# Narrow projection columns carried through V, and token records by one-hot products, in an attention and expert-routing kernel

## The reference, cut to what matters

```python
# x: (4, 256, 32, 32) -> four images of 1024 tokens, 256 channels
q, k, v = Wq x + bq, Wk x + bk, Wv x + bv            # 32, 32 and 256 rows
x = alpha * v @ softmax(q.T @ k).T + x               # per image
t = tokens(x)                                        # (4, 1024, 256)
n = layernorm(t)
prods = n @ proxy.T                                  # 16 proxies
y = cumsum(prods[..., None] * n[..., None, :], axis=tokens)
t = t + sum_p softmax(prods / 4)[p] * y[p]
n = layernorm(t)
logits = n @ gate_w.T                                # 8 experts, the best 2 of each token
top_w = softmax(top2(logits))
t = t + sum_e combine[e] * (gelu(n @ w1[e] + b1[e]) @ w2[e] + b2[e])
```

## Time and profile before

| | us |
|---|---|
| median of three runs (lowest, highest) | 883.59 (874.88, 887.9) |
| the profiled execution | 888.49 |
| its span, first to last instruction | 886.7 |
| stage A ends, stage B begins | about 219.7 |
| stage B's last residual addition (L822) begins | 386.0 |
| stage C's first layer-1 matmul | 437.95 |

### The profile page before, as it was taken

The page is one execution under the profiler, slowest core; times in us unless marked ns, Lnnn a source line. Parts: engine busy times, 40 slices in busy tenths (PEclk is TensorE's granted clock), DMA queues, the critical chain, the costliest instruction groups (busy, mean ns, idle before and its releaser), DMA issues.

```text
span 886.7 us, 18873 instructions
## 1 busy us (share of the span) xinstructions
PE 791.0 (89%) x5745; PEld 720.2 (81%) x5746; DVE 468.3 (53%) x982; ACT 324.8 (37%) x588; POOL 420.8 (47%) x405
## 2 busy tenths in 40 slices
PE   4998989897899999961299999999999999999993
PEld 3887978787567666631299999999999999999993
DVE  3777878877335365643045454454545444454541
ACT  2764747375233334220132333323233332223330
POOL 2474745456112366447324555445555544555332
PEclk9999999999655597865599999999999999999998
DMA  8576594856311111220117565265755626555222
GB/s 292 181 291 285 180 418 159 331 213 225 135 48 48 48 48 48 72 65 8 54 32 238 144 190 180 43 228 142 234 144 182 184 42 231 142 142 142 25 25 27
DMA packets 47724, 130.03 MB, mean 147 GB/s; under 512 B 7104, under 2 KB 37184, under 8 KB 43072
## 3 DMA queue, kind: packets, MB, share of 16 engines
q1 hardware_dynamic: 30288, 104.74, 31.7%
q0 software_dynamic: 16032, 19.49, 12.8%
q10 hardware_dynamic: 1360, 5.24, 1.6%
HBM read 186.52 MB, written 47.79 MB: 264 GB/s over the span
## 4 chain that ended last, share of the span: by engine, by line
PE 48%; DMA 1%; issue 1%; POOL 1%; DVE 0%; POOLq 0%; ACT 0%; DVEq 0%
PE ps_h L68 8%; PE ps_h L69 8%; PE ps_h L70 8%; PE ps_y L70 8%; PE ps_y L69 8%; PE ps_y L68 8%; PE ps_x L1331 2%; DMA out_tok<-y,to_row 0%; POOL out_tok L1218 0%; DMA records<-places 0%; DMA x_rows<-normed,from_row 0%; POOLq L1139 0%; DVE yb L1292 0%; DVE xtl L1278 0%; ACT xth L1244 0%
## 5 line engine op out<-in xcount | busy, mean ns | idle before, releaser
L1253 ACT ACTIVATE g<-ps_h,bias 128x256 f32<-128x256 f32 x288 | 120.7, 471 | 282.6 <-PE ps_h L70 282.6
L1218 POOL DMA_INDIRECT out_tok<-y,to_row x72 | 124.5, 1730 | 155.7 <-DVE y L1299 134.3
L68 PE MATMUL ps_h<-xth,wbuf 128*128 128x256 f32 x576 | 164.7, 286 | 3.3 <-issue 1.8
L68 PE MATMUL ps_y<-wbuf,gl 128*128 x576 | 165.6, 288 | 0.0
L69 PE MATMUL ps_h<-xtl,wbuf 128*128 128x256 f32 x576 | 164.4, 285 | 0.0
L70 PE MATMUL ps_h<-xth,wbuf 128*128 128x256 f32 x576 | 164.3, 285 | 0.0
L70 PE MATMUL ps_y<-wbuf,gh 128*128 x576 | 163.2, 283 | 0.0
L69 PE MATMUL ps_y<-wbuf,gh 128*128 x576 | 163.0, 283 | 0.0
L68 PEld LDWEIGHTS ps_h<-xth,wbuf 128*128 128x128 f32 x576 | 112.0, 195 | 3.9 <-issue 2.1
L69 PEld LDWEIGHTS ps_h<-xtl,wbuf 128*128 128x128 f32 x576 | 112.1, 195 | 0.0
L70 PEld LDWEIGHTS ps_h<-xth,wbuf 128*128 128x128 f32 x576 | 112.0, 194 | 0.0
(11 more groups left out here) (189 smaller groups left out, 1403.3 us busy)
## 6 DMA issues: line engine op xcount, KB each, us to landing
wbuf<-wsplit SPq DMA_DIRECT2D x71, 2048.0 KB, 8.8
wsplit<-wbuf SPq DMA_DIRECT2D x14, 2048.0 KB, 12.0
wraw<-in_w SPq DMA_DIRECT2D x16, 1024.0 KB, 7.5
xraw<-in_x_ch ACTq DMA_DIRECT2D x5, 1024.0 KB, 11.0
tok<-in_x_tok SPq DMA_DIRECT2D x1, 4096.0 KB, 17.0
out_tok<-tok SPq DMA_DIRECT2D x8, 512.0 KB
normed<-x SPq DMA_DIRECT2D x8, 512.0 KB, 2.9
x_rows<-normed,from_row POOLq DMA_INDIRECT x72, 3.2
```

The lines of the kernel that those rows point to most:

```text
L68: eng.matmul(out, ll, rh, start=first, stop=False)
L1218: pool.indirect_dma_start(out=out, out_offset=bass.IndirectOffsetOnAxis(ap=to_row[:, par, s:s + 1], axis=0), in_=y[:, par, s, :], in_offse ...
L1253: last = act.activation(g[:, f, :], ps_h[:, q, f % 2, :], ACT.Gelu_apprx_tanh, bias=bias1[:, bass.ds(e, 1), f:f + 1].rearrange("p a f -> p ...
```

## The change

**In stage A** the proxies and gates are put behind V's weights. A new `extend` multiplies Wv by the 24 proxy and gate columns, so V's projection has 304 columns: 256 of V, 24 of V times proxy and gate, and 24 of x times proxy and gate. `weigh` now has 280 columns, and `tok` 280 per tile, so that the residual addition leaves the unnormed products of each token with proxies and gates beside the token. The statistics of the first norm are taken tile by tile in stage A (`statistics(g)`, `mean_var`); since the norm is a scale and a shift of a token, the normed products are a scale of the raw ones plus a shift times column sums (`Tokens.products`, on GpSimd, in three batches of 24, 4 and 4 tiles, the third in stage B), and their softmax follows (`softmax_in`, `exponential`, `softmax_out`). Four small transfers are put ahead of the others on SyncE's queue. V's projection alternates between two PSUM regions in another order. GpSimd gets a copy per part of V.

**In stage B** the transposes of normed tokens and both projections are gone. The four images' products are turned together by two transposes (`turn`), the matrices come from one matmul of 512 columns (`attend`), and the state and output have 264 columns: the 8 gate products ride along, and the logits are those less a mean times the gates' sums (`logits`). Operands that had 16 rows or columns are padded to 128. The indirect record transfers are gone: VectorE makes one-hot tiles in bf16, 8 of 256 columns (`cell`) and 16 of 128 (`lane_tile`, `lane_part`), and TensorE adds up 16 products of them per chunk in PSUM (`record`), from which `decode` makes `records` in SBUF at the end. The shares go into `normed` as 8 more columns (GpSimd's `combine`). The counts move from VectorE to GpSimd. The chunk loop has one more round at the end.

**In stage C** the load of `places` is gone, gathered rows have 264 elements, and VectorE copies each unit's share out of them (`keep_share`).

```diff
+EXT = NP + E
+CW = C + EXT
+VW = CW + EXT
+XW = C + E
+REST = IT // 2
...
+    def products(self, pool, fixed, lo, hi, n):
...
+        pool.wait_ge(self.mv_d, n + 1)
+        pool.tensor_tensor(shift, self.mv[:, lo:hi, 0], fixed.minus_one[:, :].to_broadcast([P, m]), ALU.mult)
+        pool.tensor_tensor(inv, self.mv[:, lo:hi, 1], fixed.eps[:, :].to_broadcast([P, m]), ALU.add).then_inc(self.inv_step, 1)
+        pool.wait_ge(self.inv_step, n * 6 + 1)
+        pool.tensor_tensor(inv, inv, fixed.minus_half[:, :].to_broadcast([P, m]), ALU.pow).then_inc(self.inv_step, 1)
+        pool.wait_ge(self.inv_step, n * 6 + 2)
+        pool.tensor_tensor(shift, shift, inv, ALU.mult).then_inc(self.inv_step, 1)
+        pool.tensor_tensor(prods, prods, wide(inv, NP), ALU.mult)
+        pool.wait_ge(self.inv_step, n * 6 + 3)
+        pool.tensor_tensor(spare, each(self.sums[:, 0:NP], NP), wide(shift, NP), ALU.mult).then_inc(self.inv_step, 1)
+        pool.tensor_tensor(gated, each(self.sums[:, NP:EXT], E), wide(shift, E), ALU.mult)
+        pool.wait_ge(self.inv_step, n * 6 + 4)
+        pool.tensor_tensor(prods, prods, spare, ALU.add).then_inc(self.prods_d, 1)
+        pool.wait_ge(self.prods_d, n + 1)
+        pool.tensor_tensor(spare[:, :, 0:E], gates, wide(inv, E), ALU.mult).then_inc(self.inv_step, 1)
+        pool.wait_ge(self.inv_step, n * 6 + 5)
+        pool.tensor_tensor(gated, gated, spare[:, :, 0:E], ALU.add).then_inc(self.inv_step, 1)
+
...
+BATCHES = ((0, NT - IT), (NT - IT, NT - REST), (NT - REST, NT))
...
+            sp.dma_start(wv_nat, wv.rearrange("(k p) m -> p k m", p=P)).then_inc(ext_in, 16)
+            sp.dma_start(wv_raw[:, :, CW:CW + NP], proxy_t.rearrange("(k p) n -> p k n", p=P)).then_inc(ext_in, 16)
+            sp.dma_start(wv_raw[:, :, CW + NP:VW], gate_t.rearrange("(k p) n -> p k n", p=P)).then_inc(ext_in, 16)
+            sp.dma_start(bv_col, bv_t).then_inc(ext_in, 16)
...
                 for ch in range(4):
+                    js = slice(2 * ch, 2 * ch + 2)
                     pool.wait_ge(v_hi, done(b * 4 + ch))
-                    pool.tensor_tensor(vl[:, 2 * ch:2 * ch + 2, :], vf[:, ch % 2].rearrange("p (j c) -> p j c", j=2),
-                                       vh[:, 2 * ch:2 * ch + 2, :].bitcast(F32), ALU.subtract).then_inc(v_ok, 1)
+                    pool.tensor_copy(mine[:, js, :], vf[:, ch % 2, :, CW:VW])
+                    pool.tensor_tensor(vl[:, js, :], vf[:, ch % 2, :, 0:CW], vh[:, js, :].bitcast(F32),
...
-                        if not more and (par, part) == (1, 0):
-                            pool.wait_ge(norm_set, 3)
-                            norm1.scale_and_shift(pool, 0)
+                        if not more and par == 0:
+                            tok.products(pool, fixed, *BATCHES[part], part)
...
+                def statistics(g):
+                    wait_apart(dve, added, done(g))
+                    dve.bn_stats(tok.stat[:, bass.ds(g, 1), :].rearrange("p a c -> p (a c)"),
+                                 tok.t[:, bass.ds(g, 1), 0:C].rearrange("p a c -> p (a c)")).then_inc(tok.stat_d, 1)
...
+                def routing_weights(it):
+
+                    if it < B - 1:
+                        tok.mean_var(dve, it * IT, (it + 1) * IT, 0, it == B - 2)
+                    if it == REST:
+                        tok.mean_var(dve, *BATCHES[1], 1)
+                        tok.softmax_in(dve, *BATCHES[0], 0)
+                    if it == IT - 2:
+                        tok.softmax_out(dve, *BATCHES[0], 0)
+                        tok.softmax_in(dve, *BATCHES[1], 1)
+                    if it == IT - 1:
+                        tok.softmax_out(dve, *BATCHES[1], 1)
 
...
                 def project_v(ch):
-                    if ch == 2:
+                    if ch == 1:
                         pe.wait_ge(added, done(b * IT - 1))
-                    dst = ps_pt[1][:, ch * HALF:(ch + 1) * HALF] if ch < 2 else ps_o[ch - 2][:, :]
+                    if ch >= 2:
+                        pe.wait_ge(v_full, done(b * 4 + ch - 2))
                     for j in range(2):
+                        dst = ps_pt[1][:, j * HALF:j * HALF + VW] if ch % 2 == 0 else ps_o[:, j, 0:VW]
                         rows = slice((2 * ch + j) * P, (2 * ch + j + 1) * P)
                         for k in range(KT):
-                            last = mm3(pe, dst[:, j * C:(j + 1) * C], (xh[:, k, rows], xl[:, k, rows]),
+                            last = mm3(pe, dst, (xh[:, k, rows], xl[:, k, rows]),
                                        (wvh[:, k], wvl[:, k]), k == 0, k == KT - 1)
...
+            def prepare(c, par):
+
+                pool.wait_ge(turn_mm, done(c - 1))
+                pool.wait_ge(state_mm, done(c - 2))
+                pool.wait_ge(out_mm, done(c - 2))
+                pool.wait_ge(x1_d, done(c - 2))
+                if isinstance(c, int):
+                    pool.wait_ge(tok.weights_d, 2 if c < REST else 3)
+                else:
+                    pool.wait_ge(tok.weights_d, 3)
+                prods = chunk_of(tok.t[:, :, :], c)[:, :, C:C + NP]
+                pool.tensor_copy(prod_in[:, :, 0:NP], prods)
+                pool.tensor_copy(weight_in[:, :, 0:NP], chunk_of(tok.weights[:, :, :], c))
+                pool.tensor_copy(prod[:, par].rearrange("p (b n) -> p b n", b=B)[:, :, 0:NP], prods)
+                pool.tensor_copy(xn[:, par, :, C:XW], chunk_of(tok.gated[:, :, :], c))
+                pool.tensor_copy(inv_shift[:, par], tok.inv_shift[:, :, :].rearrange("p s (b c) -> p s b c", b=B)[
+                    :, :, :, bass.ds(c, 1)].rearrange("p s b a -> p s (b a)")).then_inc(prep_d, 1)
...
+            def mark_cells(c, par):
+
+                dve.wait_ge(spot_d, done(c))
+                dve.wait_ge(rec_mm, done(c - 2))
+                for kb in range(KB):
+                    last = dve.tensor_scalar(cell[:, par, kb, :], column_id[:, :], spot[:, 1, kb:kb + 1], None, ALU.is_equal)
+                last.then_inc(cell_d, 1)
+                wait_apart(dve, tile_d, done(c - 1))
+                for k in range(2):
+                    for b in range(B):
+                        mine = spot[:, 0, k * B + b:k * B + b + 1]
+                        dve.tensor_scalar(lane_tile[:, par, k * B + b, :], lane_id[:, :], mine, tile_no[:, b:b + 1],
+                                          ALU.is_equal, ALU.mult)
+                        last = dve.tensor_scalar(lane_part[:, par, k * B + b, :], lane_id[:, :], mine, part_id[:, 0:1],
+                                                 ALU.is_equal, ALU.mult)
...
-            def scatter(c, par):
-
-                wait_apart(pool, record_d, done(c))
-                for k, b in [(k, b) for k in range(2) for b in range(B)]:
-                    pool.indirect_dma_start(
-                        out=places, out_offset=bass.IndirectOffsetOnAxis(ap=place[:, par, k, b:b + 1], axis=0),
-                        in_=record[:, par, k, b, :], in_offset=None).then_inc(record_out[par], 16)
...
+                then(dve.tensor_copy(number[:, :], ps_rec[:, CELLS:2 * CELLS]), 1)
+                dve.scalar_tensor_tensor(out=empty[:, :], in0=ps_rec[:, 0:CELLS], scalar=0.0, in1=padding_id[:, :],
+                                         op0=ALU.is_equal, op1=ALU.mult)
+                then(dve.scalar_tensor_tensor(out=number[:, :], in0=ps_rec[:, 0:CELLS], scalar=float(P), in1=number[:, :],
+                                              op0=ALU.mult, op1=ALU.add), 2)
+                then(dve.scalar_tensor_tensor(out=records[:, 0:CELLS], in0=number[:, :], scalar=float(P), in1=empty[:, :],
+                                              op0=ALU.subtract, op1=ALU.add), 3)
...
+            def attend(c, par):
+                pe.wait_ge(turned_d, done(c))
+                pe.wait_ge(attn_d, done(c - 1))
+                pe.matmul(ps_a[:, :], prod_t[:, par], weight_t[:, par].rearrange("p b t -> p (b t)"),
+                          start=True, stop=True).then_inc(a_mm, 1)
+                pe.wait_ge(x1_d, done(c))
+                pe.wait_ge(state_d, done(c - 1))
...
+            def record(c, par):
+
+                pe.wait_ge(lane_d, done(c))
+                pe.wait_ge(cell_d, done(c))
+                for kb in range(KB):
+                    end = isinstance(c, int) and c == CH - 1 and kb == KB - 1
+                    pe.matmul(ps_rec[:, 0:CELLS], lane_tile[:, par, kb, :], cell[:, par, kb, :], start=False, stop=False)
+                    last = pe.matmul(ps_rec[:, CELLS:2 * CELLS], lane_part[:, par, kb, :], cell[:, par, kb, :],
+                                     start=False, stop=end)
+                last.then_inc(rec_mm, 1)
+
...
+                if exists(i - 2):
+                    record(i - 2, par)
+                if exists(i + 1):
+                    attend(i + 1, 1 - par)
+                if exists(i + 2):
+                    turn(i + 2)
```

882 lines of the change are left out of this document (482 added, 400 removed).

## The result

The changed kernel takes 832.4 us (median of 4 runs, 831.3 to 834.8) beside 880.9 for the kernel before (4 runs, 874.9 to 887.9). The ratio is 0.945, with a 95% interval of 0.937 to 0.953: faster. Its sign was right, its size was a third of what came.

What follows compares the result with a forecast made beforehand. It took TensorE's own work to bound four of five stretches, and latency the tail. Stage A +25.9, fill −1.8, periods −25, tail −16.3 and stage C 0 sum to −17.2: 883.59 to 866 us, range 844 to 892.

Steps and rivals of the forecast that it cites:

- the mechanism of the last image: Stage A's end: GpSimd's products delay a weight subtraction, so the reload and ScalarE's high half come 11.3 later; +13.3 us.
- the steps of the tail: Last residual addition to stage C's first matmul: one-hots, places, records, table, decoding, gather; 35.6 us for 51.95.
- the middle between 94: Stage B's seven periods: the clock decides between 94 and 136 us, so 115 was taken for 140.1.
- my warm rival: Stage B: dense record and score matmuls hold 2.4 GHz; periods 94, total 845 us; chance 0.14.
- VectorE's 94: Stage B at full clock: VectorE needs 13.4 us a chunk and TensorE waits on it; seven periods 94.
- my upper bound of 6.5: Stage B: 24 one-hots a chunk on VectorE at 0.27 us each, as for float32 scalings; 3.3 was taken.
- My lower bound: Stage B: one-hots cost VectorE 1.7 us a chunk, at the tier table's four elements a cycle.
- TensorE has no slack in these: Stage A: added columns in `weigh` and V's matmuls show in full, 3.2 us an image, +9.7 for three images.
- my 2.1 and my 0: Stage A: added `weigh` columns cost 2.1 us an image, or 0 if something other than columns sets the pace.
- Fill (−1.8 forecast: Stage B's start: the first chunk's new chain takes 24.4 us for 26.2, output 9.3 of it at low clock.
- Cold clock: Stage B stays at 1.2 GHz: periods 136, tail 2 longer, total 889 us; chance 0.16.
- held-up one-hots: Stage B: GpSimd's small operations hold up VectorE's one-hots, which then cost the upper bound; total 883 us; chance 0.12.

Runs made afterwards that it cites:

- e2: Changed kernel with the 16 one-hots of 128 lanes of each chunk made twice, the second time into an unread buffer: 862.7 us.
- e3: Changed kernel with the second matmul of each image's output taking only that image's 16 rows instead of 128: 835.5 us.
- e5: Kernel before the change, with turned products, turned weights and state padded by zero rows from 16 to 128: 857.0 us, ratio 0.968.
- e10: Changed kernel with scores ahead of records, count ahead of the last ones, and ScalarE scaling plain lane one-hots that VectorE makes: 824.1 us.
- e6: Changed kernel with `weigh` given back its 256 columns, V's projection keeping the added ones: 831.9 us.
- e12: Changed kernel with products early, scores ahead of records, count ahead of the last ones, and the weights' buffer allocated ahead of the tokens' buffers: 814.0 us.
- e8: Changed kernel with GpSimd making the eight lane one-hots scaled by the tile's number, VectorE the other eight: 854.4 us.
- e4: Changed kernel with 24 TensorE matmuls of zeros before the wait for the one-hots: 829.7 us.
- e9: Changed kernel with the next chunk's scores and state ahead of the records, and the expert count ahead of the last records: 822.2 us.

## Why the prediction was wrong

**The bound now, and which stretches the change touches: right.** So were the order of events, the mechanism of the last image, the steps of the tail, and VectorE as the bound at full clock. Four of five terms had the right sign. Forecast and result differ by 38.6 in the profiled executions; 26.8 of it are the seven periods. Of my signs, ScalarE's wait (11.66), the tail (37.9) and the missing transfer of `places` came about as forecast; the additions came every 13.7 and not every 16 to 17, and a granted clock of 0.9 in stage B, one of my signs of being wrong, came (0.90).

**Periods (115 forecast, 88.3 measured).** The step that failed is the middle between 94, VectorE's chunks at full clock, and 136, TensorE's at half clock. It gave TensorE half of the periods as their bound, and that is 21 of the 26.8. What the runs showed is VectorE as the bound of every period with one-hots (e2), at a mean granted clock of 0.90. The 94 itself was 5.7 too high. Three sizes stand behind this.

The first is TensorE's price. I read 1.14 and 0.62 as the price of a matmul "with 128-wide weights" and 0.88 as that of one with 16-wide ones, and gave the state's matmuls, whose weights are now padded, the dearer price. It is the other way round. The dear ones in the earlier trace rows alternate between weights of 16 rows and of 128; the cheap ones are of one kind. e3 and e5 show it from both sides: 0.64 with the alternation, 0.43 to 0.44 without, at half clock 1.14 and 0.85. Since the change gives all of them 128 rows, every price that I used was too high: for a cold chunk 8 x 1.17 and 4 x 1.17 instead of some 0.87 each, 3.6 less; at full clock 2.1 less. The diff shows the padding, and I counted it only against the change. In the changed kernel, though, this price matters little by itself: with the alternation put back the periods are 90.3 (e3).

The second is the clock. I took the middle between a chunk at half clock and one at full clock, since nothing told me more. TensorE's granted clock came out at 0.90, and at 0.87 in the chunk above, where half clock covers the gap and the first 2.8 us of the records. The condition of my warm rival, that dense record matmuls hold the clock, came in part: they start at half clock after the gap, and full clock returns during them. No run took them away, so their share is not known. e5 shows that padding the 16 rows takes the kernel before from 0.68 to 0.92.

The third is VectorE's 94, seven chunks of 13.4. A full chunk takes 13.7, so the chunk was right, but by luck, since two errors cancel: the one-hots cost 5.2 a chunk (8 x 0.20 for the cells, 16 x 0.22 for the lanes) and not 3.3, which is nearer my upper bound of 6.5; and VectorE is idle 1.6 in it and not 3.5, since it has the next chunk's work between its dependent steps. What was too high is the number of chunks: the first period has no one-hots and takes 7.3, the second 12.3. I had left such chunks out of TensorE's sum and not out of VectorE's.

The rule of the tier table in the Trainium skill ("VectorE: DVE Perf Modes", the perf-mode tier table), four bf16 elements a cycle, isn't refuted by this: from 128 to 256 columns a plain comparison goes from 0.17 (e10) to 0.20. The columns are cheap. What I missed is a part that does not shrink with the columns, 0.13 by an estimate from these two rows, and 0.05 on top for a second operation with its pointer (0.22 for 0.17). My lower bound was 1.7, for which I named no row, and the measured cost is three times that.

**Stage A (+25.9 forecast, +21.6 measured).** The start is 2.4 for 1.9. Three images cost 6.8 (53.56 less 51.29, three times) where columns and boundaries were put at 10.7. Here the step "TensorE has no slack in these" failed: in a tile it had 0.34 us of slack, and e6 puts `weigh`'s part at 0.92 an image. For `weigh` alone that lies midway between my 2.1 and my 0. The clock goes with the rest: from first addition to first addition the three images grew by 0.7, 3.1 and 3.1, and the granted clock at the boundary behind each was 1.00, 0.94 and 0.89 (78:90, 131:144, 184:198) where it had been 0.95, 1.00 and 1.00 (75:87, 127:138, 178:188.5). How much of the 6.8 it makes is not shown. The last image is the term that I took for the largest, and it held: 12.4 for 13.3, with ScalarE's wait at 11.66. Some of that is luck. The reload landed 5.4 after the subtraction (221.6 to 226.95) where I had carried over the old 7.1, and from there to the end it took 14.7 where I had 12.8, with VectorE held up, for which I had no term. Inside it the power took 4.20 for 24 elements, nearly per element, where I took the middle.

**Fill (−1.8 forecast, −7.6 measured).** The same wrong prices and the clock: scores, state and output were put at 16.0, while they took 8.9 (250.72 to 259.6). The output, forecast at 9.3, ran at full clock in 3.6.

**Tail (−16.3 forecast, −14.1 measured).** Step by step 11.3, 6.9, 3.5, 4.9, 1.7 and 9.4 for 11.2, 5.2, 3.9, 4.9, 1.7 and 8.7. The 1.7 in the second are the one-hots again.

**Stage C (0 forecast, −3.9 measured).** Its 3,596 matmuls have the same clock and count, but start 0.118 to 0.119 apart in `ps_y` where it was 0.120. It repeats: 448.8 and 449.2 in the two traces of the old form, 444.5 to 445.8 in all those of the new one. 1,728 `ps_y` matmuls at 0.0018 or so less each are some 3 of the 3.9. That operands lie at other places of SBUF in the two forms is the likely cause, since e12 shows that such a place moves these prices by 0.0009 to 0.0014; that it is the cause here is not shown.

**The rivals.** Warm clock was the nearest in its sum (845), and its reason is shown only in part. Cold clock and held-up one-hots did not come: beside GpSimd's one-hots those of VectorE last 0.32 for 0.30 (e8). The hold that I feared is real, but it falls on VectorE's operations with two SBUF inputs, and in stage A. Nor does every GpSimd operation cause it: L545 takes 0.16 at 210.22, in the middle of GpSimd's power of 4.20. As a whole the range failed because the periods were given 94 as their lowest, which counts seven full chunks, and because the fill and stage C added 5.8 and 3.9 that no bound allowed for.

## What to carry to other kernels

Ask of a price read between two neighbours in a trace what the neighbour is: a matmul that follows one of another row count pays for it, and padding short operands with zeros to 128 rows can be more than half of a gain. Where an engine that waits in order has independent work behind the wait, put that work ahead of it; two such exchanges were worth 10 us here, and the periods' clock came back to 1.00 as well. When a stretch has a first and a last chunk without some of the work, take that out of every engine's sum. Before work is put on GpSimd between two long instructions, follow what waits for the second, and which VectorE operations with two SBUF inputs will meet it.

## What the runs showed of the hardware

The granted clock of TensorE did not follow its busy share alone. With float32 matmuls of 16 and of 128 rows in turn it stood at 0.68 over 140 us of which TensorE was busy 98%; with 128 rows throughout at 0.92, busy 88% (e5). In the changed kernel 16 rows in half of the output matmuls give 0.81 for 0.90 (e3). Whether it is the rows or their alternation is open, and with the same matmuls the kernel before also had 12 us at 1.00. The Trainium skill ("TensorE: Matmul & The Clock Gate", HAM oscillation) puts the fall of the clock down to gaps in TensorE's work. The gap of 3.75 us in each chunk bears that out, since filling or shortening it gave 1.00 (e4, e9). The stretches of the kernel before at half clock and without a gap (258:270, TensorE busy 12.00 of 12.00) go beyond it, and here the measurement decides.

A float32 matmul of 256 or 264 columns costs 0.43 to 0.44 at full clock behind one of the same rows and 0.62 to 0.64 behind one of other rows; at half clock 0.85 and 1.14.

GpSimd needs 0.81 for a one-hot of 128 bf16 elements (VectorE 0.22), and for a power 1.02 with 4 elements and 4.20 with 24.

The place of an operand in SBUF moved the start-to-start time of equal matmuls by about 1% (e12: 0.1200 to 0.1186 and 0.1180 to 0.1189).
